# Where the transpose of a context chunk stands in SyncE's program during cross-attention

## The reference

```
x = layernorm(x + self_attention(x))                  # single head, width 256
Q = x Wq^T + bq;  K = ctx Wk^T + bk
A = softmax(Q K^T / sqrt(1024))                       # 112 x 375 for each sequence
x = layernorm(x + A ctx)                              # the values are the context itself
x = layernorm(x + ffn(x))                             # 1024 -> 2752 -> 1024, 4-bit weights
```

## Time and profile before

| | us |
|---|---|
| median of 3 runs (lowest, highest) | 1929.4 (1928.26, 1933.14) |
| the profiled execution's own time | 1929.76 |
| its span, first to last instruction | 1928.0 |
| PE busy, share of the span | 1817.8, 94% |
| DVE busy, share of the span | 857.5, 44% |
| PE idle in front of matmuls, ended by an SBUF to SBUF DMA | 24.2 in 14 times |

### The profile page before, as it was taken

How to read it: one execution, slowest core, us unless ns; L and a number is a source line. 1 busy time by engine, 2 the same in 40 slices (tenths; PEclk the granted TensorE clock), 3 DMA queues, 4 the chain that set the end, 5 groups by cost and what they waited for, 6 DMA issues and landing times.

```text
span 1928.0 us, 26581 instructions
## 1 busy us (share of the span) xinstructions
PE 1817.8 (94%) x10186; PEld 1022.5 (53%) x10186; DVE 857.5 (44%) x1326; ACT 445.2 (23%) x676; POOL 394.2 (20%) x278
## 2 busy tenths in 40 slices
PE   4888899898999869999999999999999999999998
PEld 2666644586877735454445444444545444444443
DVE  5688550666887844434443444344343310111111
ACT  3222110444555532222222222222222200000000
POOL 0212378233343321111111111111111100000000
PEclk9999999999999989999999999999999999999999
DMA  9243561699999942212212111212121321221220
GB/s 312 67 131 99 151 196 44 133 212 238 231 231 227 236 91 59 45 35 59 44 35 54 40 44 35 60 35 44 38 55 40 112 89 66 102 102 61 91 102 22
DMA packets 298812, 196.10 MB, mean 102 GB/s; under 512 B 258368, under 2 KB 272768, under 8 KB 296580
## 3 DMA queue, kind: packets, MB, share of 16 engines
q1 hardware_dynamic: 292516, 192.19, 39.2%
q10 hardware_dynamic: 6240, 3.15, 0.6%
HBM read 105.11 MB, written 50.34 MB: 81 GB/s over the span
## 4 chain that ended last, share of the span: by engine, by line
PE 55%; issue 24%; DVE 7%; DMA 6%; SPq 5%; POOL 2%; ACT 1%; POOLq 0%; DVEq 0%; ACTq 0%
PE psum L1294 53%; SPq L1717 4%; DMA arena<-arena 3%; DMA arena<-in_x 2%; DVE arena L713 1%; POOL small L932 1%; PE psum L1496 1%; POOL arena L941 1%; PE psum L1514 1%; DMA x_parts_scratch<-arena 1%; PE psum L1287 1%; DVE arena L820 1%; DVE arena L497 1%; DMA arena<-in_L_xattn_Wq 1%; DVE small L412 0%
## 5 line engine op out<-in xcount | busy, mean ns | idle before, releaser
L1294 PE MATMUL psum<-arena 128*128 128x448 f16 (+7 forms) x9404 | 1748.1, 347 | 51.5 <-DMA arena<-arena 24.2
L1294 PEld LDWEIGHTS psum<-arena 128*128 128x128 f16 (+3 forms) x9404 | 972.5, 107 | 808.0 <-issue 94.0
L1048 POOL TENSOR_TENSOR arena<-arena 128x1024 f16<-128x1024 f32 (+1 forms) x64 | 136.1, 2126 | 662.2 <-ACT arena L1236 662.2
L874 DVE SCALAR_TENSOR_TENSOR arena<-psum,small,arena 128x448 f32<-128x448 f32 x84 | 57.4, 684 | 412.9 <-PE psum L1294 412.9
L914 DVE SCALAR_TENSOR_TENSOR arena<-psum,small,arena 128x512 f32<-128x512 f32 x28 | 21.0, 751 | 327.4 <-PE psum L1294 327.4
L932 POOL TENSOR_TENSOR small<-small 112x1 f32<-112x1 f32 (+1 forms) x46 | 50.9, 1107 | 507.8 <-DVE small L386 507.8
L1236 ACT ACTIVATE arena<-arena 128x1024 f16<-128x1024 f32 (+1 forms) x65 | 68.7, 1057 | 276.8 <-DVE arena L860 276.8
L1249 ACT ACTIVATE arena<-arena 128x448 f16<-128x448 f32 (+1 forms) x88 | 50.7, 577 | 290.3 <-DVE arena L874 290.3
L1006 POOL TENSOR_TENSOR arena<-arena 128x224 f16<-128x224 f32 x64 | 56.2, 879 | 126.4 <-ACT arena L1149 126.3
L858 DVE TENSOR_TENSOR arena<-arena,psum 128x1024 f32<-128x1024 uint32 x65 | 79.4, 1221 | 2.6
L880 DVE TENSOR_TENSOR arena<-arena 128x448 f16<-128x448 f32 (+1 forms) x88 | 55.0, 625 | 57.1 <-ACT arena L1249 57.1
(11 more groups left out here) (182 smaller groups left out, 769.3 us busy)
## 6 DMA issues: line engine op xcount, KB each, us to landing
h_scratch<-arena SPq DMA_DIRECT2D x84, 224.0 KB, 2.7
arena<-h_scratch SPq DMA_DIRECT2D x13, 1376.0 KB, 6.0
arena<-in_ctx SPq DMA_DIRECT2D x32, 512.0 KB, 5.5
arena<-in_x SPq DMA_DIRECT2D x32, 448.0 KB, 5.7
x_scratch<-arena SPq DMA_DIRECT2D x32, 448.0 KB, 3.4
arena<-in_L_ffn_down_qweight SPq DMA_DIRECT2D x21, 512.0 KB
x_parts_scratch<-arena SPq DMA_DIRECT2D x16, 448.0 KB, 5.5
arena<-in_ctx SPq DMA_DIRECT2D x16, 448.0 KB
```

The source lines that it names most:

```text
L874: dve.scalar_tensor_tensor(h_f[0:n, :], up[0:n, :], sc_u[0:n, :], g_act[0:n, :], ALU.mult, ALU.mult).then_inc(s_hf, 1)
L1048: pool.tensor_tensor(dst[1], src, dst[0], ALU.subtract).then_inc(s_wl, 1)
L1294: mm = pe.matmul(out, a, r, start=(k == 0), stop=(k == len(pairs) - 1))
```

## The change

In a step of the cross-attention SP now issues the transpose of chunk c - 1 of n + 1 right behind the read of chunk c of n + 2, and the last transpose at the end. The order read 0, store, read 1, read 2, transpose 0, 1, 2 becomes read 0, store, read 1, transpose 0, read 2, transpose 1, transpose 2. The wait for the slot (`s_l`, in step 0 `s_v`) moves ahead of read 1. The semaphore `s_due`, for which nobody waits, is raised twice in a step and not once. No other engine's program changes.

```diff
@@ cross_attention of block.sync, inside "for c in range(CC)"
                         if c == 0 and not known(n, 1):
                             store_x2(n - 1, (b + 1) % 2)
+                            sp.wait_ge(s_l, n)
+                        elif c == 0:
+                            sp.wait_ge(s_v, 2 * NG)
+                        if c < 2:
+                            sp.sem_inc(s_due, 1)
+
+                        if has(1) and c:
+                            load_cxt(c - 1, (b + 1) % 2)
                     if has(1):
-                        if not known(n, 1):
-                            sp.wait_ge(s_l, n)
-                        else:
-                            sp.wait_ge(s_v, 2 * NG)
-                        sp.sem_inc(s_due, 1)
-                        for c in range(CC):
-                            load_cxt(c, (b + 1) % 2)
+                        load_cxt(CC - 1, (b + 1) % 2)
```

## The result

| | before | after |
|---|---|---|
| median, us (lowest to highest; ten runs each) | 1928.8 (1924.6 to 1935.2) | 1940.5 (1934.1 to 1945.2) |
| ratio, 95% interval | | 1.0055 [1.004, 1.007] |
| profiled execution: own time, span, us | 1929.8, 1928.0 | 1940.9, 1939.2 |

The medians lie 11.7 us apart; the ratio, which has the interval, is worth 10.6 us. The forecast was 1922.4 in 1909 to 1937. The time lies above the range, between the mild form of the slower rival (1936) and its full form (1944).

A forecast was written before the change was run, and what follows sets the result against it. The loop was taken as bound by a circle through PE's waits on SBUF transposes. Nine steps at 0.7 us (6.3) plus 1.5 for the last, 7.8 together, less up to 1 for the semaphore, gave 1929.4 - 7 = 1922.4, range 1909 to 1937.

The forecast's parts named there:

- the slower rival: SP stands in transpose 0, so chunk 2's read is late for DVE; full form 1944, mild form 1936; chance 0.17.
- What bounds the loop: Slices nine to fourteen: DMA at nine tenths, PE waits 24.2 us on transposes; behind them PE bounds, so loop gains stay.
- Nothing for the semaphore and the moved wait: On SP: the extra increment counted as nothing, at most 1.6 us; the moved slot wait costs nothing.
- The circle that takes over: Through chunk 2's read and DVE's largest of it: 18.4 to 19.7 us a step, against 19.6 now.
- d: Time transpose 0 holds SP's queue at its new place, taken as 3.4 to 3.8 us.
- The first steps: Steps before the nine, with transposes from HBM in the queue: taken as 0, between gain 1 and loss 2 for each of three.
- the last step: The loop's last step has no reads, so only gain is left: 1.5 us taken of PE's 1.96 us wait.
- What comes off the path: Between low part of chunk 2 and last transpose: transpose 0 leaves, freeing at most its 3.79 us on SP's queue.
- The hole that transpose 0 was to fill: DMA engines idle 3.2 us from 600.8 to 604.0, while read 2 waits for its low part.
- the second rival: Nothing moves: queue served in order, transpose 2 lands as before, DVE loses what transpose 0 gains; 1925 to 1933, chance 0.26.
- the full gain: The hole swallows transpose 0, reads of chunk 2 not late, PE's 24 us of waits go; 1905 or 1902, chance 0.12.
- wrong towards slower: Profile signs: transpose 0 of 5 us or more, DVE's read waits over 40, PE idle moved to line 1382 or `attended`.

The follow-up runs named there:

- its control: The kernel before with reads of chunks 0 and 1 cut to 256 of 1024 columns from the third sequence on; 1922.9 us, ratio 0.9962.
- the short reads: The changed kernel with reads of chunks 0 and 1 cut to 256 of 1024 columns from the third sequence on; 1916.1 us, ratio 0.9923.

## Why the prediction failed

**What bounds the loop** held in the main: 8.5 of the 11.2 us lie in the loop, and PE's slices behind it are unchanged. One reading was off without harm: in the first slice behind the six named, PE stands at six and the DMA at four, and only from the next on at nine and at one or two.

**Nothing for the semaphore and the moved wait** held, at 1.0005 [0.9988, 1.0023].

**The circle that takes over** held. With the measured d and the measured 4.8 us of the read it gives 10.4 + 0.4 + 4.86 + 4.8 = 20.5 us a step, and the trace has 20.3; the part that was taken as 10.0 to 10.8, from the largest of chunk 2 to the next read 1, measures 10.1. The point from which it decides, d above about 4.2, agrees with the two kernels on its sides: 4.86 loses 0.55%, about 3.1 gains against its control. In the arithmetic one slip stands: the middle of 18.4 to 19.7 is 19.05 and not 18.9, so the sum itself gave a gain of some 0.55 us a step, 5 in nine steps and not 6.3.

**The step that failed is d**, "nearer to 3.79 than to the ends; I take 3.4 to 3.8". It measured 4.86. Two reasons were given there. One was the nearest row; but 3.79 is a transpose behind a read of 448 KB, ahead of which SP had issued nothing for 2.5 us, and the new place is behind a read of 512 KB, a store and another read of 512 KB, issued within 2.4 us. The row of 5.79, set aside as the case with transposes from HBM, was as near. The other was that "the copies meet a freer queue" because the transposes of the step before finish earlier; they don't, as the table of the set's times shows. The 1.1 to 1.5 us by which d was too small are 10 to 13 us in nine steps, more than the 7 us of gain. With the right d the same sum has a circle of 19.9 to 20.8, in the middle 20.3 against 19.6, and gives 1929.4 + 9 x 0.7 - 1.5 (the last step) = 1934: slower, but still 6 us short of the median.

**The first steps**, taken at nothing, are a part of these 6 us. From one line 674 to the next, the five steps ahead of the nine are 3.9 us longer in all than before (105.6, before 101.7). The nine are 6.5 longer, and the last is 1.9 shorter, near the 1.5 foretold: together the 8.5 us of the loop. The other 2.7 us are those outside it.

**What comes off the path** failed too, and deeper. I took it that transpose 0, once moved, frees "at most its 3.79 us" on the way to the last transpose. With DVE's wait for read 2 taken away the circle through read 2 was gone, and that way alone should have shown the gain. It showed none: 0.9997 [0.9984, 1.001]. The hole that transpose 0 was to fill is the only long one in nine steps of before; I had seen two steps and taken it for half of them. The reading that fits the runs, though none isolates it, is that the last transpose lands when the DMA engines have done the work of the step. The time on SP's queue that I had counted is in large part that of the copies in front, and moves with them: transpose 0 holds SP for 1.8 us in the mean with no copy in front, 3.1 behind the short reads and 4.9 behind the full ones. This is what the second rival said ("the same bytes stand ahead of transpose 2 as before"). I had weighed it as one outcome at 0.26; it is the state of things beneath the others. The rule of the Trainium skill that I set beside it ("DMA: Bandwidth & Descriptors", section "Queues, rings and completion order": each DMA engine takes a ring's descriptors in order) would have given no change at best, and agrees with this trace in its direction: what transpose 0 gains, read 2 loses. The other rule of the Trainium skill (the same page, "Rules for kernel authors"), to issue early, would have given the full gain, and the trace is against it here.

**The expected signs in the profile.** Right: the place of transpose 0; PE's wait for the transposes down (7.5, foretold 12); DVE's wait up; the hole of 3.2 us gone (the longest stretch of the nine steps without a packet is 1.4). Wrong: transpose 0 of 4.9 us and not 3.4 to 3.8, the reads 1.5 to 3.5 us behind their low part and not 0.5 to 2, a step of 20.3 and not 18.9. The three signs named for "wrong towards slower" are there: transpose 0 of about 5 us, DVE's waits above 40, PE's idle time at line 1382. The last sign, `logits` waiting as long as before while transpose 0 comes earlier, is not in the changed kernel but in the one without the wait for read 2, and there it points where it was to point, to the DMA engines and not to SP.

**The slower rival** had place, chain and point right. Its full form (d 5.8, 1944) was too strong and its mild one (d 5, 1936) 4.5 us short of the median. Its chance of 0.17 was too low: the argument set against it, that the chain of transposes would finish as early as now and leave PE without a new wait, overlooked that PE's new wait comes by way of DVE and line 1382.

**What stays open.** Which resource of the DMA engines makes the set take 17 to 18 us isn't settled: the share stands near 1 while the rate varies between 71 and 375 GB/s. What makes the 2.7 us outside the loop isn't either. Nor is it settled why a read on ScalarE's queue lands so late beside transposes on SP's; that the two queues are served in turns would fit, but is only argued. No version that was run beats the kernel before with the whole work done.

## What to carry to other kernels

A DMA that is moved forward in an in-order queue moves everything behind it back, so follow each transfer that it passes to its reader, and that reader's queue to the engine that sets the time; here the passed read had no slack, and the moved transpose had nothing to win. Price the moved DMA by the bytes that stand in front of it at its new place, not by its time at the old one. Before you count on an idle stretch of the DMA engines, look for it in every step and not in one. When a wait is taken away by moving an instruction, run the same move on the kernel before: twice here the move cost as much by itself as what it was to measure.

## What the hardware showed that I had not expected

- The same 128 x 2048 half-precision transpose between two places in SBUF holds its queue 1.7 to 2.0 us with nothing issued just in front, about 3 behind two quarter-size reads and a store, and 4.3 to 5.3 behind two reads of 512 KB and a store (ten steps of one execution each).
- A read of 448 KB, issued 2.6 us sooner after its low part but on ScalarE's queue, arrives later: 9.2 us from issue to its reader beside SP's transposes, where 4.8 were needed on SP's queue.
- On one queue, the order of four copies, a store and three transposes changes the time of the whole set by no more than 1 us in 18, which is also what kernels with the same order differ by.
